# First attention of a fused transformer kernel: value products of four heads issued together in four 32-column groups

## The chip, the cores and the metric

The kernel runs on one core of one Trainium2 chip as one launch. The metric is the device time of that launch in microseconds (us), as a median of runs; lower is better.

## The reference, cut to what matters

The program is a four-layer model over 8 sequences (batches) of T = 333 tokens and width 256. An image tokeniser makes the first 256 tokens, 77 text tokens are appended, and four attention-like and four feed-forward-like layers follow. The change touches only the first attention, 16 heads of width 16, dense softmax, no mask:

```python
h = jnp.concatenate([h, txt], axis=1)
h = h + _L0_attn_ref(_layernorm(h, axis=-1), L0_attn_ln_g, L0_attn_ln_b, L0_attn_Wq, L0_attn_bq, ...)
# per batch and head:  softmax(q k^T / sqrt(16)) v      (q, k, v: 333 x 16)
```

## The kernel before, in words

Every engine runs its own instruction list, and the lists wait for one another through counted semaphores (`wait_ge`, `then_inc`). The first attention is the function `attention16`. The 333 tokens are three tiles of 111 (`NT = 3`), the 16 heads are 8 pairs (`NPAIR`), so a batch has `NS = 24` steps. In a step `s`, TensorE (PE), VectorE (DVE) and ScalarE (ACT) work on one pair and one tile each:

- `scores`, L719: PE writes query-by-key scores of a pair to one of two `psS` buffers, `AHEAD = 9` steps before they are needed.
- `largest`, L554: DVE reduces them to the row maximum into `mx`. After six steps a `most` piece turns the maxima on PE (L702) and DVE makes `mT` out of them (`mhigh` L580, `mT` L582).
- `scores_less_most`, L731 and L734: PE computes the turned scores (keys by queries) and adds minus the maximum, into the single buffer `psT`. When `s % 6 == 0` it first waits for the `most` piece of its four heads. It always waits for the `exp` of the step before.
- `exp`, L653: ACT reads `psT` and writes probabilities to `PT`.
- `values`, L745: PE multiplies the probabilities with `vS` and accumulates in `psO`, 32 output columns to a head. One float32 product is two MATMUL records in the trace, so a step's two heads are four. `out` (L657, ACT) copies `psO` after four heads.

Between these, PE works off *pieces* that all share the one buffer `psM`: `x` (L687, turned input of the next batch), `qk` (L691, projections), `v` (L697), `most` (L702), `ot` (L706, turned output). A piece on PE waits until its predecessor was read out of `psM` (`piece_out`). ACT reads out `x` and `qk`; DVE reads out `v` (L575), `most` (L580, L582) and `ot` (L586, L589). Their places among the steps are a list written out by hand:

```python
AT = [(1, "x", 0), (2, "x", 1), (3, "qk", 0), (4, "qk", 1), (5, "most", 1), (6, "ot", 3), (7, "qk", 2),
      (8, "qk", 3), (9, "ot", 0), (11, "most", 2), (12, "v", 0), (13, "v", 1), (15, "ot", 1), (17, "most", 3),
      (21, "ot", 2), (23, "most", 0)]
```

The first batch has no `("ot", 3)`; the last has only `most` 1 to 3 and `ot`. Batches 1 to 6 run in a hardware loop of three rounds with two batches each. DVE's list for a step is unchanged by the diff and reads:

```python
if s + AHEAD < NS or not last:
    largest(*of(b, p, s + AHEAD)[::2])
for args in pieces(b, p, s, first, last):
    piece(*args)
```

Of the kernel before, what the change touches and what calls it, by code (L numbers as in the profile page):

```python
# [21 lines left out]
ACT = mybir.ActivationFunctionType  # L22
# [3 lines left out]
T = 333  # L26
TT = 111
NT = 3
# [337 lines left out]
def attention16(nc, sh):  # L366
# [5 lines left out]
    H, DH = 16, 16  # L372
    NPAIR = 8
    NS = NPAIR * NT
    TE = T + 1
    HIGH = -4096
    AHEAD = 9
    with ExitStack() as ctx:
        sb = lambda name, shape, dt=F32: ctx.enter_context(nc.sbuf_tensor(name, shape, dt))
# [15 lines left out]
        spread = sb("spread", [128, 2, TT], F32R)  # L395
        sign = sb("sign", [128, 2])
        less = sb("less", [128, 1])
        PT = [sb(f"PT{i}", [TT, 2, NT, T]) for i in range(2)]
        oS = sb("oS", [128, T])
        rec = sb("rec", [TT, NT, 4])  # L400
        tmp = sb("tmp", [TT, NT, 4, DH])
# [54 lines left out]
        def some(n):  # L456

            return not isinstance(n, int) or n > 0

        def of(b, p, s):  # L460

            return (b, p, s) if s < NS else (b + 1, 1 - p, s - NS)

# [167 lines left out]
        @block.scalar  # L631
        def _(act):
            s_ = nc.scalar

            def piece(kind, j, b, p, n):
                if kind == "x":
                    act.wait_ge(piece_done, n + 1)
                    s_.activation(xT[:, j, :], psM[:, 0:T], ACT.Identity, bias=sh.col("a_b", j),
                                  scale=sh.col("a_g", j)).then_inc(piece_out, 1)
                if kind == "qk":  # L640
                    act.wait_ge(piece_done, n + 1)
                    if some(4 * b + j - 1):
                        act.wait_ge(low_ready, 4 * b + j - 1)
                    bias, scale = (bq4[:, j // 2:j // 2 + 1], DH ** -0.5) if j % 2 == 0 else (sh.col("a_bk", j // 2), 1.0)
                    s_.activation(raw[j % 2][:, :], psM[:, 0:T], ACT.Identity, bias=bias,
                                  scale=scale).then_inc(piece_out, 1)

            def exp(b, s):
                jp, a = s // NT, s % NT
                act.wait_ge(st_done, NS * b + s + 1)  # L650
                if a == 0 and some(NPAIR * b + jp - 1):
                    act.wait_ge(pv_done, NPAIR * b + jp - 1)
                s_.activation(PT[jp % 2][:, :, a, :], psT[0:TT, :, 0:T], ACT.Exp).then_inc(exp_done, 1)  # L653

            def out(b, g):
                act.wait_ge(pv_done, NPAIR * b + 2 * g + 2)
                s_.activation(oS[:, :], psO[:, 0:T], ACT.Copy).then_inc(o_out, 1)  # L657

            act.wait_ge(consts, 3)
            for n, (kind, j) in enumerate(START):  # L660
                piece(kind, j, 0, 0, n)

            def body(b, p, first, last):
                for s in range(NS):
                    if s == 1 and not first:
                        out(b - 1, 3)
                    if s % 6 == 1 and s > 1:
                        out(b, s // 6 - 1)
                    for args in pieces(b, p, s, first, last):
                        piece(*args)  # L670
                    exp(b, s)
                if last:
                    out(b, 3)
            batches(act, body)

        @block.tensor
        def _(pe):
            mm = nc.tensor.matmul

            def piece(kind, j, b, p, n):  # L680
                if some(n):
                    pe.wait_ge(piece_out, n)
                if kind == "x":
                    if j == 0:
                        pe.wait_ge(xn_ready, b + 1)
                    for t in range(NT):
                        r = nc.tensor.transpose(psM[:, qt(t)], xn[:, t, 128 * j:128 * j + 128], sh.ident[0:TT, 0:TT])  # L687
                if kind == "qk":
                    at = 128 * (j // 2)
                    for c in range(KT):  # L690
                        r = mm(psM[:, 0:T], sh.wt("a_q" if j % 2 == 0 else "a_k", c, at, at + 128), xT[:, c, :],  # L691
                               start=c == 0, stop=c == KT - 1)
                if kind == "v":
                    for t in range(2 * j, min(2 * j + 2, NT)):
                        at = D * (t % 2)
                        for c in range(KT):
                            r = mm(psM[0:TT, at:at + D], xT[:, c, qt(t)], sh.wt("a_v", c, 0, D),  # L697
                                   start=c == 0, stop=c == KT - 1, skip_group_check=True)
                if kind == "most":
                    pe.wait_ge(mx_ready, 4 * b + j + 1)  # L700
                    for t in range(NT):
                        r = nc.tensor.transpose(psM[:, qt(t)], mx[j % 2][:, t, :], sh.ident[0:TT, 0:TT])  # L702
                if kind == "ot":
                    pe.wait_ge(o_out, 4 * b + j + 1)
                    for t in range(NT):
                        r = nc.tensor.transpose(psM[0:TT, 128 * t:128 * t + 128], oS[:, qt(t)], sh.ident[:, :])  # L706
                r.then_inc(piece_done, 1)

            def scores(b, p, s):

                jp, t = s // NT, s % NT
                if t == 0 and jp % 4 == 0:
                    for n in (jp // 2, jp // 2 + 1):
                        pe.wait_ge(stack_in[n], 128 * (b + 1))
                if some(NS * b + s - 1):
                    pe.wait_ge(max_done, NS * b + s - 1)
                for half in range(2):
                    ph = slice(64 * half, 64 * half + 64)
                    r = mm(psS[s % 2][0:TT, half, 0:TE], qs[p][ph, jp, qt(t)], ks[p][ph, jp, :], start=True, stop=True)  # L719
                r.then_inc(s_done, 1)  # L720

            def scores_less_most(b, p, s, first, last):

                jp, a = s // NT, s % NT
                if s % 6 == 0:
                    pe.wait_ge(piece_out, most_place(b, jp // 2, first, last) + 1)
                if some(NS * b + s):
                    pe.wait_ge(exp_done, NS * b + s)
                for half in range(2):
                    ph = slice(64 * half, 64 * half + 64)  # L730
                    mm(psT[0:TT, half, 0:TE], ks[p][ph, jp, qt(a)], qs[p][ph, jp, :], start=True, stop=False)  # L731
                for half in range(2):
                    ph = slice(64 * half, 64 * half + 64)
                    r = mm(psT[0:TT, half, 0:TE], spread[ph, jp % 2, :], mT[jp // 2 % 2][ph, :], start=False, stop=True)  # L734
                r.then_inc(st_done, 1)

            def values(b, p, s):
                jp, a = s // NT, s % NT
                pe.wait_ge(exp_done, NS * b + s + 1)
                if s % 6 == 0 and some(4 * b + jp // 2):  # L740
                    pe.wait_ge(o_out, 4 * b + jp // 2)
                for half in range(2):
                    h = 2 * jp + half
                    at = 32 * (h % 4)
                    r = mm(psO[at:at + 32, 0:T], vS[p][:, a, h, :], PT[jp % 2][:, half, a, :], start=a == 0,  # L745
                           stop=a == NT - 1)
                if a == NT - 1:
                    r.then_inc(pv_done, 1)

            for n, (kind, j) in enumerate(START[:-1]):  # L750
                if n == 0:
                    pe.wait_ge(consts, 3)
                piece(kind, j, 0, 0, n)
            for s in range(AHEAD):
                scores(0, 0, s)
            piece("most", 0, 0, 0, N0 - 1)

            def body(b, p, first, last):
                for s in range(NS):
                    if s + AHEAD < NS or not last:  # L760
                        scores(*of(b, p, s + AHEAD))
                    if s >= 2:
                        values(b, p, s - 2)
                    elif not first:
                        values(b - 1, 1 - p, NS + s - 2)
                    for args in pieces(b, p, s, first, last):
                        piece(*args)
                    scores_less_most(b, p, s, first, last)
                if last:
                    values(b, p, NS - 2)  # L770
                    values(b, p, NS - 1)
                    piece(*tail())
            batches(pe, body)


# [2268 lines left out]
```

## Time and profile before

| | us |
|---|---|
| median of three runs | 2289.98 (2289.2 to 2295.62) |
| the profiled execution, its own time | 2287.08 |
| its span in the trace | 2285.3 |
| PE busy (matmul) | 1807.9, 79% of the span |
| DVE busy | 1140.6, 50% |
| ACT busy | 759.1, 33% |

PE is TensorE's matmul stream and PEld its weight loads. A row of the timeline has the start in us from the start of the span, the duration in us, engine, source line, operation, output<-inputs with shapes, and how many instructions were merged into it; in brackets stands how long the engine was idle before and what released it. Matmul ends are modelled, so the start of the next instruction is the better measure of when PE was free. PEclk is the granted TensorE clock as a share of 2.4 GHz. The first attention's steps run from about 167 us to 540 us.

### The profile page before, as it was taken

How to read it: one execution, taken by the hardware profiler on the slowest of the kernel's cores; microseconds unless marked ns; L12 is line 12 of the kernel's file. 1: busy time of each engine (PE TensorE's matmuls, PEld its weight loads, DVE VectorE, ACT ScalarE, POOL GpSimd, SP SyncE). 2: the span in 40 equal slices, each digit the busy share in tenths (PEclk: the TensorE clock that was granted, in tenths of full speed). 3: DMA queues.
4: the chain of work that ended last, by engine and by line, in shares of the span. 5: the costliest groups of instructions: out<-in, count | busy, mean ns of one | idle time of the engine just before them, and what ended most of it. 6: DMA issues, size and time to landing. Idle time of an engine off the chain costs nothing. (4 is left out here: it accounts for less than half of the span.)

```text
span 2285.3 us, 32329 instructions
## 1 busy us (share of the span) xinstructions
PE 1807.9 (79%) x9490; PEld 1178.8 (52%) x9490; DVE 1140.6 (50%) x3699; ACT 759.1 (33%) x1873; POOL 502.2 (22%) x728
## 2 busy tenths in 40 slices
PE   0049999998897989777763999768888888882998
PEld 0024444444665667554541677535666555661676
DVE  5346767673326766744552222156665666641111
ACT  0004444453231245221210221137555566630211
POOL 0130100001101122301111111114434444531122
PEclk9999999998997999899885999859998999995999
DMA  8444544444200000160000101030000010002332
GB/s 179 133 79 89 106 81 87 72 72 121 84 18 0 1 1 1 39 257 12 12 13 24 33 30 33 26 106 9 16 17 19 24 25 19 19 19 59 129 135 70
DMA packets 72299, 129.65 MB, mean 57 GB/s; under 512 B 23030, under 2 KB 59573, under 8 KB 67442
## 3 DMA queue, kind: packets, MB, share of 16 engines
q1 hardware_dynamic: 52636, 107.80, 18.1%
q0 software_dynamic: 17632, 14.26, 2.5%
q10 hardware_dynamic: 1893, 5.99, 0.8%
q8 instruction: 56, 0.92, 0.2%
q14 instruction: 82, 0.67, 0.1%
HBM read 89.79 MB, written 39.52 MB: 57 GB/s over the span
## 5 line engine op out<-in xcount | busy, mean ns | idle before, releaser
L2304 POOL TENSOR_SCALAR l_P<-l_P,l_ri 111x111 f32<-111x111 f32 (+1 forms) x256 | 178.3, 714 | 159.3 <-DVE l_ri L2492 158.4
L653 ACT ACTIVATE PT<-psT 111x666 f32<-111x666 f32 x192 | 139.4, 726 | 156.4 <-PE psT L734 156.0
L2586 ACT ACTIVATE l_P<-l_S,l_nm 111x111 f32<-111x111 f32 (+2 forms) x384 | 179.3, 471 | 32.7 <-DVE l_nm L2485 32.5
L554 DVE TENSOR_REDUCE mx<-psS 111x2 f32<-111x666 f32 x192 | 159.6, 847 | 25.7 <-PE psS L719 25.7
L745 PE MATMUL psO<-PT,vS 111*32 111x333 f32 x768 | 147.0, 461 | 0.1
L2706 PE MATMUL l_psP<-ident,l_P 111*111 111x111 f32 x768 | 108.8, 281 | 32.2 <-DVE l_PT L2501 27.6
L2706 PEld LDWEIGHTS l_psP<-ident,l_P 111*111 111x111 f32 x768 | 95.4, 189 | 62.9 <-issue 33.1
L2042 DVE COPY t_hT<-t_psG 128x512 f32<-128x512 f32 x56 | 36.1, 686 | 175.0 <-PE t_psG L2085 175.0
L2485 DVE CUSTOM_DVE_ANT_0 l_S<-l_psA,l_am 111x111 f32<-111x111 f32 (+1 forms) x256 | 79.0, 331 | 76.9 <-PE l_psA L2692 70.1
L2074 PE MATMUL t_psH<-expert_w,t_xT 128*128 x224 | 103.4, 606 | 1.5 <-DVE t_xT L2035 1.2
L2097 PE MATMUL t_psY<-expert_w,t_hT 128*128 x448 | 101.4, 379 | 0.6 <-ACT t_yb L2007 0.6
L2595 ACT ACTIVATE l_P<-l_P,l_ri 111x333 f32<-111x333 f32 x128 | 66.2, 565 | 90.5 <-DVE l_ri L2492 90.4
L2718 PE MATMUL l_psO<-l_PT,l_vS 111*64 111x333 f32 (+2 forms) x768 | 95.8, 388 | 0.6 <-ACT l_oT L2600 0.6
L521 POOL TENSOR_TENSOR low<-raw,high 128x333 f32<-128x333 f32 x32 | 28.6, 895 | 307.6 <-DVE high L566 307.6
L2677 PE MATMUL l_psM<-l_wo,l_oT 128*111 128x256 f32 x384 | 87.7, 381 | 8.5 <-ACT l_oT L2600 7.5
L106 DVE BATCH_NORM_STATS2 moments<-h 111x6 f32<-111x256 f32 (+1 forms) x192 | 69.1, 416 | 42.0 <-DMA h<-h_scratch 36.5
L2097 PEld LDWEIGHTS t_psY<-expert_w,t_hT 128*128 128x128 f32 x448 | 82.9, 190 | 11.1 <-issue 1.0
L2928 PE MATMUL c_psY<-c_w,c_hT 128*111 128x256 f32 x384 | 84.2, 379 | 0.6 <-DVE c_yb L2875 0.6
L687 PE MATMUL psM<-ident,xn 111*128 111x111 f32 x48 | 10.6, 343 | 92.7 <-DVE spread L611 82.5
L2911 PE MATMUL c_psH<-c_xT,c_w 128*128 128x333 f32 x256 | 76.8, 459 | 8.6 <-DVE c_xT L2861 6.5
L731 PE MATMUL psT<-qs,ks 64*111 64x334 f32 x384 | 79.4, 409 | 3.2 <-DVE mT L582 0.7
L2718 PEld LDWEIGHTS l_psO<-l_PT,l_vS 111*64 111x64 f32 x768 | 53.6, 148 | 52.0 <-issue 19.2
(401 smaller groups left out, 3744.4 us busy)
## 6 DMA issues: line engine op xcount, KB each, us to landing
expert_w<-in_moe_dram SPq DMA_DIRECT2D x8, 2048.0 KB, 24.6
c_w<-in_moe_dram SPq DMA_DIRECT2D x16, 1024.0 KB, 7.2
qs<-halves_scratch SPq DMA_DIRECT2D x128, 83.5 KB, 3.2
ks<-halves_scratch SPq DMA_DIRECT2D x128, 83.5 KB, 4.1
halves_scratch<-high SPq DMA_DIRECT2D x32, 167.0 KB, 3.0
halves_scratch<-low SPq DMA_DIRECT2D x32, 167.0 KB, 3.6
c_xb<-xs_scratch SPq DMA_DIRECT2D x8, 667.3 KB
xs_scratch<-zeros SPq DMA_DIRECT2D x6, 777.0 KB
```

The lines of the kernel that those rows point to most:

```text
L554: v.tensor_reduce(mx[J % 2][:, t, c:c + 65:64], psS[s % 2][0:TT, :, 0:T], AX.X, ALU.max, negate=True).then_inc(max_done, 1)
L653: s_.activation(PT[jp % 2][:, :, a, :], psT[0:TT, :, 0:T], ACT.Exp).then_inc(exp_done, 1)
L731: mm(psT[0:TT, half, 0:TE], ks[p][ph, jp, qt(a)], qs[p][ph, jp, :], start=True, stop=False)
L745: r = mm(psO[at:at + 32, 0:T], vS[p][:, a, h, :], PT[jp % 2][:, half, a, :], start=a == 0, stop=a == NT - 1)
L2074: r = mm(psH[s % 2][q][:, :], xT[s % 2][:, k, :], experts.w[:, e, 1024 * k + 512 * q:1024 * k + 512 * q + 512], start=k == 0, stop=k == KT ...
L2097: r = mm(psY[:, 0:D], hT[s % 2][:, c, :], experts.w[:, e, at:at + D], start=c == 0, stop=c == 7)
L2304: r = g.tensor_scalar(Pt, Pt, ri[:, c % 2, 2 * t + half:2 * t + half + 1], None, ALU.mult)
L2586: s_.activation(P[c % 4][:, half, at(t):at(t + 1)], Sm[:, half, at(t):at(t + 1)], ACT.Exp, bias=nm[:, c % 2, i:i + 1], scale=-1.0, accum_o ...
L2677: r = mm(psM[0:TT, 0:D], oT[p][:, c, qt(j)], wo[:, c, :], start=c == 0, stop=c == NC - 1)
L2706: r = nc.tensor.transpose(psP[0:TT, half, qt(i)], P[c % 4][:, half, at(t) + TT * a:at(t) + TT * a + TT], sh.ident[0:TT, 0:TT])
L2718: r = mm(psO[64 * half:64 * half + 64, TT * a:T], vS[p][:, a, DH3 * kv:DH3 * kv + DH3], PT[c % 2][:, half, a, TT * a:T], start=a == 0, sto ...
L2928: r = mm(psY[t % 2][0:TT, 0:D], hT[p][:, f, qt(t)], stream.w[p][:, at:at + D], start=f == 0, stop=f == NF - 1)
```

## The change

`values` no longer runs once in a step for two heads and one key tile, but once in two steps for four heads and one key tile: eight MATMUL records into the four 32-column groups of `psO`. For that, a batch's steps are renumbered on the exp side: `parts(s)` makes even and odd steps the first and second pair of the same four heads on the same key tile, where before the three tiles of one pair followed each other. `PT` becomes three buffers (one to a tile) of two pairs each. Semaphore counts follow. PE's order in a step changes too: before it was scores, values, pieces, scores less most; now it is pieces, scores less most, scores, and values in even steps. ACT's and DVE's orders stay.

```diff
+    NQ = NS // 2
-        PT = [sb(f"PT{i}", [TT, 2, NT, T]) for i in range(2)]
+        PT = [sb(f"PT{i}", [TT, 2, 2, T]) for i in range(NT)]
+        def parts(s):
+            return 2 * (s // 6) + s % 2, s % 6 // 2
...
             def exp(b, s):
-                jp, a = s // NT, s % NT
+                jp, a = parts(s)
                 act.wait_ge(st_done, NS * b + s + 1)
-                if a == 0 and some(NPAIR * b + jp - 1):
-                    act.wait_ge(pv_done, NPAIR * b + jp - 1)
-                s_.activation(PT[jp % 2][:, :, a, :], psT[0:TT, :, 0:T], ACT.Exp).then_inc(exp_done, 1)
+                if some(NQ * b + s // 2 - 2):
+                    act.wait_ge(pv_done, NQ * b + s // 2 - 2)
+                s_.activation(PT[a][:, jp % 2, :, :], psT[0:TT, :, 0:T], ACT.Exp).then_inc(exp_done, 1)
             def out(b, g):
-                act.wait_ge(pv_done, NPAIR * b + 2 * g + 2)
+                act.wait_ge(pv_done, NQ * b + NT * g + NT)
...
-            def values(b, p, s):
-                jp, a = s // NT, s % NT
-                pe.wait_ge(exp_done, NS * b + s + 1)
-                if s % 6 == 0 and some(4 * b + jp // 2):
-                    pe.wait_ge(o_out, 4 * b + jp // 2)
-                for half in range(2):
-                    h = 2 * jp + half
-                    at = 32 * (h % 4)
-                    r = mm(psO[at:at + 32, 0:T], vS[p][:, a, h, :], PT[jp % 2][:, half, a, :], start=a == 0,
-                           stop=a == NT - 1)
-                if a == NT - 1:
-                    r.then_inc(pv_done, 1)
+            def values(b, p, u):
+                J, a = u // NT, u % NT
+                pe.wait_ge(exp_done, NS * b + 2 * u + 2)
+                if a == 0 and some(4 * b + J):
+                    pe.wait_ge(o_out, 4 * b + J)
+                for c in range(2):
+                    for half in range(2):
+                        n = 2 * c + half
+                        r = mm(psO[32 * n:32 * n + 32, 0:T], vS[p][:, a, 4 * J + n, :], PT[a][:, c, half, :],
+                               start=a == 0, stop=a == NT - 1)
+                r.then_inc(pv_done, 1)
...
                 for s in range(NS):
-                    if s + AHEAD < NS or not last:
-                        scores(*of(b, p, s + AHEAD))
-                    if s >= 2:
-                        values(b, p, s - 2)
-                    elif not first:
-                        values(b - 1, 1 - p, NS + s - 2)
                     for args in pieces(b, p, s, first, last):
                         piece(*args)
                     scores_less_most(b, p, s, first, last)
+                    if s + AHEAD < NS or not last:
+                        scores(*of(b, p, s + AHEAD))
+                    if s % 2 == 0:
+                        if s >= 2:
+                            values(b, p, s // 2 - 1)
+                        elif not first:
+                            values(b - 1, 1 - p, NQ - 1)
```

## Rows read from the trace of the kernel before

**Rows 1.** Windows view, first attention: us, busy per engine (instructions), PEclk, DMA share, GB/s.
```profile
170.00:538.00 368.00, 355.40 (x2305) 167.33 (x2301) 253.75 (x607) 171.97 (x262) 32.13 (x42) 0.98 0.43 79
```

**Rows 2.** Timeline of a step without a piece, then the next one's start.
```profile
504.87 0.41 PE L731 MATMUL psT<-qs,ks 64*111 64x334 f32 x2
...
505.11 0.32 PE L734 MATMUL psT<-mT,spread 64*111 64x334 f32 x2
...
505.26 0.32 PE L719 MATMUL psS<-ks,qs 64*111 64x334 f32 x2
505.47 0.73 ACT L653 ACTIVATE PT<-psT 111x666 f32<-111x666 f32 x1 [0.66 <-PE psT L734]
...
505.51 0.75 PE L745 MATMUL psO<-PT,vS 111*32 111x333 f32 x4
505.62 0.85 DVE L554 TENSOR_REDUCE mx<-psS 111x2 f32<-111x666 f32 x1 [0.26 <-PE psS L719]
...
506.25 0.41 PE L731 MATMUL psT<-qs,ks 64*111 64x334 f32 x2
```

**Rows 3.** Timeline of the last batch's end, where no scores are left.
```profile
536.15 0.40 PE L731 MATMUL psT<-qs,ks 64*111 64x334 f32 x2
...
536.63 0.75 PE L745 MATMUL psO<-PT,vS 111*32 111x333 f32 x4
...
537.52 0.17 PEld L731 LDWEIGHTS psT<-qs,ks 64*111 64x111 f32 x2 [0.75 <-ACT PT L653]
```

**Rows 4.** PE's timeline over batch 6: each kind of piece, and a batch's period.
```profile
450.90 0.75 PE L745 MATMUL psO<-PT,vS 111*32 111x333 f32 x4
451.59 0.58 PE L706 MATMUL psM<-ident,oS 128*111 128x128 f32 x3
452.10 0.41 PE L731 MATMUL psT<-qs,ks 64*111 64x334 f32 x2
...
454.80 0.50 PE L702 MATMUL psM<-ident,mx 111*128 111x111 f32 x3
...
456.71 0.41 PE L731 MATMUL psT<-qs,ks 64*111 64x334 f32 x2
...
464.20 1.39 PE L691 MATMUL psM<-xT,w 128*128 128x333 f32 x4
...
480.69 1.98 PE L697 MATMUL psM<-w,xT 128*111 128x256 f32 x8
...
483.93 1.12 PE L697 MATMUL psM<-w,xT 128*111 128x256 f32 x4
...
502.11 0.40 PE L731 MATMUL psT<-qs,ks 64*111 64x334 f32 x2
```

**Rows 5.** Timeline of steps 5 and 6: a `most` piece, then an `ot` piece.
```profile
324.22 0.41 PE L731 MATMUL psT<-qs,ks 64*111 64x334 f32 x2
...
324.32 0.51 DVE L580 TENSOR_SCALAR mhigh<-psM 128x333 int32<-128x333 int32 x1
...
324.91 0.57 DVE L582 SCALAR_TENSOR_TENSOR mT<-psM,less,mhigh 128x333 fp32r<-128x333 f32 x1
...
325.60 0.57 PE L706 MATMUL psM<-ident,oS 128*111 128x128 f32 x3
...
326.22 0.23 DVE L586 RECIPROCAL rec<-psM 111x12 f32<-111x12 f32 x1
...
326.53 0.49 DVE L589 TENSOR_TENSOR tmp<-psM,rec 111x64 f32<-111x64 f32 x3
```

**Rows 6.** Timeline of step 12: DVE reads out the first `v` piece.
```profile
482.71 0.76 DVE L575 TENSOR_TENSOR vS<-psM,rows 111x256 f32<-111x256 f32 x2 [1.33 <-PE psM L697]
```

**Rows 7.** Timeline after the hardware loop's second round began, TensorE at its low clock.
```profile
312.96 1.32 PE L745 MATMUL psO<-PT,vS 111*32 111x333 f32 x4
```

**Rows 8.** Windows view, two stretches of later stages with PE partly idle.
```profile
580.00:590.00 10.00, 7.15 (x24) 5.17 (x25) 2.71 (x2) 3.70 (x8) 2.25 (x1) 0.83 0.19 78
...
670.00:680.00 10.00, 6.79 (x24) 4.31 (x24) 2.47 (x3) 3.03 (x6) 0.00 (x0) 1.00 0.00 0
```

More of the change, by code:

```diff
@@ L722, in scores_less_most @@
             def scores_less_most(b, p, s, first, last):
-                jp, a = s // NT, s % NT
+                jp, a = parts(s)
                 if s % 6 == 0:
@@ L735, in scores_less_most @@
                 r.then_inc(st_done, 1)
-            def values(b, p, s):
-                jp, a = s // NT, s % NT
-                pe.wait_ge(exp_done, NS * b + s + 1)
-                if s % 6 == 0 and some(4 * b + jp // 2):
-                    pe.wait_ge(o_out, 4 * b + jp // 2)
-                for half in range(2):
-                    h = 2 * jp + half
-                    at = 32 * (h % 4)
-                    r = mm(psO[at:at + 32, 0:T], vS[p][:, a, h, :], PT[jp % 2][:, half, a, :], start=a == 0,
-                           stop=a == NT - 1)
-                if a == NT - 1:
-                    r.then_inc(pv_done, 1)
+            def values(b, p, u):
[9 more added lines that the diff above has]
+                r.then_inc(pv_done, 1)
             for n, (kind, j) in enumerate(START[:-1]):
@@ L768, in body @@
                     scores_less_most(b, p, s, first, last)
+                    if s + AHEAD < NS or not last:
[5 more added lines that the diff above has]
+                            values(b - 1, 1 - p, NQ - 1)
                 if last:
-                    values(b, p, NS - 2)
-                    values(b, p, NS - 1)
+                    values(b, p, NQ - 1)
                     piece(*tail())
```

## The prediction

> **What bounds the kernel now.** I read the busy shares by window first: in the first attention PE is busy 355.4 of 368 us and DVE 253.8 [rows 1], at a granted clock of 0.98 [rows 1]. That looks like a plain PE bound, so I read the timeline step by step, because a step has two limits that happen to meet. I time a step from one L731 to the next.
>
> The first limit is PE's own work [rows 2]: L731 to L734 0.24 us, to the scores L719 0.15, to the values L745 0.25, together 0.65; then the values. In front of a piece the values hold PE for 0.69 us (450.90 to 451.59) [rows 4]. A piece is worth its listed duration less 0.07, as the next instruction starts that much before the modelled end (`ot` 0.58 listed, 0.51 to the next) [rows 4]: `x` and `most` 0.44 (both are three turns of 111 columns), `ot` 0.51, `qk` 1.32, `v0` 1.91, `v1` 1.05.
>
> The second limit is the turn between PE and ACT over the one buffer `psT` [rows 2]: L731 starts at 504.87, exp at 505.47 (0.60 later), runs 0.73, and the next L731 follows at 506.25, 0.05 after its end. That is 1.38 us, whatever else PE does. The end of the last batch shows it alone: no scores are left there, PE is done with the values at 536.63 + 0.69 = 537.32, and still the next L731 waits for ACT until 537.52, 1.37 us after the one before [rows 3]. So a step without a piece is bound by exp's turn, with PE's 0.65 + 0.69 = 1.34 just underneath; a step with a piece is bound by PE. A middle batch takes 502.11 - 456.71 = 45.4 us [rows 4]. Eight steps of 1.38 and sixteen of 1.34 plus their piece (2 `x`, 4 `qk`, 4 `most`, 4 `ot`, 2 `v` = 12.9) give 45.4, so the two limits explain the batch.
>
> **The change part by part (times are for a middle batch).**
>
> *Values in four groups.* Two heads take 0.75 us for four records with a mean near 0.46, so two groups do run side by side, in two passes of about 0.28. Four groups are not in the trace. Lower bound 0.69 (all hidden), upper bound 0.69 + 2 x 0.28 = 1.25 (two and two). I take 0.75, near the lower, since the second group adds no pass of its own: the added 0.06 is for four more starts.
> The Trainium skill's "TensorE: Matmul & The Clock Gate" (section Measured speedup vs the span model) gives about 4 ns to a further tile of a packed group; by that the block would be 0.70, and the sum below 4 us lower (an estimate).
>
> *What the saved blocks are worth.* In an odd step no values stand on PE any more. It needs 0.40 + about 0.26 plus the next piece. But exp's 1.38 stays, so a step without a piece gains nothing: the twelve saved blocks are mostly turned into PE idle time. It pays only where a piece that is done before an even step is PE-bound now: s = 1 (`x1`) 1.78 to 1.38, s = 3 and 7 (`qk`) 2.66 to 1.98. Gain 0.40 + 2 x 0.68 = 1.8. Eleven of sixteen pieces stand in front of odd steps, right behind the values of an even one, and gain nothing; nine of these pay the 0.06 of the larger block (s = 0, 2, 4, 8, 10, 14, 16, 20, 22), and s = 18 0.03: cost 0.6.
> A rule that speaks against the change stands in "TensorEngine Tiling (Array Packing)" of the Trainium skill (PSUM Bottleneck): tiling makes TensorE faster but not the reading out of PSUM. The trace agrees, with 1.38 us for exp's turn.
>
> *PE's new order against DVE's old one.* This is the term that decides. DVE's list of a step is largest(s+9), then piece(s). Before, PE issued scores(s+9) ahead of piece(s), so that reduction was done or running when the piece came. Now scores(s+9) comes after the piece and after L731/L734. DVE, in order, can't read out piece(s) until those scores are there and reduced. From L731 of step s: scores start at 0.40, the reduction 0.36 after that (505.26 to 505.62) and takes 0.85 [rows 2]: 1.61 us. Only then comes the piece's read-out, which before began 0.1 us after L731 (324.22 to 324.32) [rows 5]. Where something on PE waits for that read-out soon, PE stalls:
>
> - `most`: `mhigh` to the end of `mT` is 1.16 us (324.32 to 325.48) [rows 5]. Ready at 1.61 + 1.16 = 2.77. A next `psM` piece starts 0.12 later (325.60), at 2.89. An L731 that waits for `mT` starts 0.21 after it: at s = 23 the step takes 1.47 now (454.80 + 0.44 to 456.71) [rows 4], of which 0.10 and 1.16 are before the end of `mT`. So 2.98.
> - s = 17 and 23: the next L731 has s % 6 = 0 and waits for `mT`. 1.47 to 2.98, +1.51 each.
> - s = 5: `ot3` waits for `psM`, 2.89 + 0.51 = 3.40, before 1.34 + 0.51 = 1.85: +1.55.
> - s = 11: `v0` waits, 2.89 + 1.91 = 4.80, before 1.34 + 1.91 = 3.25: +1.55.
> - s = 6: `qk2` waits for `ot3`'s read-out, 0.80 us (326.22 to 327.02) [rows 5]: 1.61 + 0.80 + 0.12 + 1.32 = 3.85, before 2.66: +1.19.
> - s = 12: `v1` waits for `vS`, 0.76 [rows 6]: 1.61 + 0.76 + 0.12 + 1.05 = 3.54, before 2.39: +1.15. Its larger values block is covered here, as in s = 6.
>
> Together 8.5. The other `ot` pieces have two or more steps before the next piece: covered. `x` and `qk` are read out by ACT, whose order against PE stays.
>
> *Buffers and waits.* exp waits for values two groups back, out waits for the last block of its four heads, which ends some 1.4 us into an even step, and its 0.45 us are over by 1.9, before the odd step's exp can start at 1.98. Nothing. If that cover went, 0.4 us four times a batch. The `scores` keep 8 steps of lead; their reduction waits for no one else.
>
> Sum for a middle batch: 8.5 + 0.6 - 1.8 = +7.3, six times: 43.8. The first batch has no `ot3`: s = 5 still waits for `mT` (+1.51), s = 6 doesn't stall: 3 x 1.51 + 1.55 + 1.15 + 0.6 - 1.8 = +6.0. The last has no `x`, `qk`, `v`, and from s = 15 no reduction ahead of the piece: s = 5 (+1.5), s = 11 (+1.5), and 0.1: +3.1. Where TensorE is at its low level (1.2 GHz) behind a loop boundary and at the start, a values block costs 1.25 instead of 0.69 [rows 7]; one of the two blocks goes in three such places, and the piece steps gain some 1 us each: -3. Total 43.8 + 6.0 + 3.1 - 3 = +49.9.
>
> The profiled execution is 2287.1, so 2337.0; the median of the runs is 2.9 above it: about **2340 us**, 2.2% slower.
>
> **The rivals.**
>
> *PE's busy time is what counts (faster).* If exp's turn were shorter than 1.38 when PE is idle, and DVE's late read-outs found slack, each batch would lose twelve blocks of 0.69 less twelve times 0.06: 7.6 us, 60 us in all: 2230. For it: PE's 97% share [rows 1]. Against it: the 1.37 with PE idle [rows 3]. It needs both to hold; it decides once the stalls are under what the lighter PE saves.
> By the skill's "TensorE: Matmul & The Clock Gate" (the small-M row of its table) column groups give 2.38 times for three tiles; that speedup is of PE alone.
>
> *No change.* DVE's late read-out is hidden by something that I don't see, exp's turn stays: -1.8 + 0.6 a batch, about -10 at most: 2280 to 2290.
>
> *Four groups run two and two.* Ten even steps a batch pay 0.5 more: +5 a batch, 40 in all: 2381.
>
> *The clock.* After the change PE idles for some 2.2 us in s = 5, 11, 17 and 23, and in most odd steps 0.7. Elsewhere a window with 7.15 of 10 us busy was granted 0.83, one with 6.79 busy 1.00 [rows 8]. So dips can come or not. A dip of 3.4 us (0.83 over 10 us) makes about 1.5 us of loss, by 1.32 against 0.75 for the values [rows 7, 4]; two a batch 24 us: 2365.
>
> **How the numbers follow.** Chances: forecast 0.70, two and two 0.09, clock 0.11, no change 0.04, faster 0.06. About 0.3% (7 us) is what can be told from no change here. Slower by more: 0.90; within: 0.04; faster: 0.06. The range takes the forecast with each stall up to a third smaller (8.5 to 5.7, about 20 us: 2320) up to two-and-two with a few dips, 2388.
>
> **What would show it.** Right: a batch's period of L731 near 52.7 us; DVE's `mhigh` 1.6 us after L731 instead of 0.1; idle PE before L706, L697, L691 and L731 released by DVE `mT`, `tmp`, `vS`, about 50 us more than now; steps without a piece still 1.38; exp count and duration unchanged. Wrong: `mhigh` right behind its piece; no-piece steps below 1.38; L745's eight records spanning more than 1 us; PEclk well below 0.98 over the stage. The code's order on DVE is the thing I lean on most; the four-group block is the least known size.

## The result and the profile after

The changed kernel takes 2398.6 us (median of four, 2386.8 to 2405.1) against 2292.4: a ratio of 1.0457, 95% interval 1.041 to 1.0504. Slower, as forecast, but by 106 us and not by 50, and above the stated range (up to 2388). The profiled execution is 2401.9 us, span 2400.2.

The profile's page gives the granted clock in 40 slices of 60 us, in tenths. Slices 3 to 11 hold the first attention:

```profile
PEclk9988777878599899999886699977998999986999
```

The windows view from the first L736 (the L731 of before) of the first attention to the last; columns as in [rows 1]:

```profile
165.73:646.16 480.43, 374.18 (x2315) 191.83 (x2315) 256.94 (x612) 175.44 (x264) 32.11 (x42) 0.76 0.33 61
```

The same stretch of before, cut at the same two instructions, is 370.2 us. So nearly all of the difference (110 of 115 us of span) is in this stage. Its mean granted clock fell from 0.98 [rows 1] to 0.76, which is about half of the time at the low level of 1.2 GHz.

The timeline of two steps at the high level: first step 20 of the seventh batch, then its step 23, which ends with the wait of step 0 of the last batch. L724 are the scores, L750 the values, L711 an `ot` piece and L707 a `most` piece:

```profile
587.41 0.41 PE L736 MATMUL psT<-qs,ks 64*111 64x334 f32 x2 [0.67 <-ACT PT L658]
...
588.05 0.77 PE L750 MATMUL psO<-PT,vS 111*32 111x333 f32 x8
588.75 0.58 PE L711 MATMUL psM<-ident,oS 128*111 128x128 f32 x3
```
```profile
591.97 0.51 PE L707 MATMUL psM<-ident,mx 111*128 111x111 f32 x3
592.40 0.40 PE L736 MATMUL psT<-qs,ks 64*111 64x334 f32 x2
...
592.79 0.31 PE L724 MATMUL psS<-ks,qs 64*111 64x334 f32 x2
...
593.92 0.50 DVE L585 TENSOR_SCALAR mhigh<-psM 128x333 int32<-128x333 int32 x1
594.49 0.57 DVE L587 SCALAR_TENSOR_TENSOR mT<-psM,less,mhigh 128x333 fp32r<-128x333 f32 x1
...
595.11 0.40 PE L736 MATMUL psT<-qs,ks 64*111 64x334 f32 x2 [2.00 <-DVE mT L587]
```

Eight records in four column groups hold PE for 0.70 us (588.05 to 588.75), no longer than four did in two [rows 4]. And `mhigh` begins 1.52 us after L736, where it was 0.10 [rows 5]: PE is idle for 2.00 us until `mT` is there.

The same kind of steps at the low level, in the sixth batch (steps 22 and 23):

```profile
533.19 1.34 PE L750 MATMUL psO<-PT,vS 111*32 111x333 f32 x8
534.46 0.82 PE L707 MATMUL psM<-ident,mx 111*128 111x111 f32 x3
...
535.21 0.62 PE L736 MATMUL psT<-qs,ks 64*111 64x334 f32 x2
...
538.38 0.62 PE L736 MATMUL psT<-qs,ks 64*111 64x334 f32 x2 [2.00 <-DVE mT L587]
```

The same work takes PE 1.5 to 1.8 times as long as above: 0.62 for 0.41 (L736), 0.82 for 0.51 (L707), 1.34 for 0.77 (L750). The wait for `mT` is 2.00 us at either level. The waits from 160 to 650 us (waiting engine and line, what it waited for: us, times, longest):

```profile
DVE mx L559 <- PE psS L724: 184.4, 152, 4.0
...
PE psT L736 <- DVE mT L587: 33.6, 17, 2.1
...
PE psT L736 <- ACT PT L658: 28.4, 45, 0.9
...
PE psM L711 <- DVE mT L587: 14.3, 7, 2.1
PE psM L702 <- DVE mT L587: 14.0, 7, 2.0
```

DVE waits for the scores that now come late, and PE waits for DVE. In the stage of before, DVE waited for the scores for 24.7 us, PE waited for `mT` only once, for 0.7 us, and for ACT's exp once, for 0.2.

All of this is best read as step lengths, L736 to L736, steps 0 to 23 of the fifth batch, worked out from the timelines (the last row is e3, experiment 4 below; each length can be off by 0.01):

```
before  1.76 1.76 2.65 2.64 1.75 1.84 2.64 2.64 1.83 1.38 1.76 3.23 2.38 1.39 1.85 1.38 1.75 1.47 1.46 1.38 1.84 1.38 1.75 1.47 = 45.4
after   3.12 1.84 3.44 2.12 1.77 3.23 4.88 3.56 1.84 1.39 1.78 4.62 3.37 1.37 1.85 1.38 1.77 2.72 1.46 1.54 3.29 1.71 3.13 3.14 = 60.3
filled  1.78 1.40 2.67 2.11 1.78 3.22 3.67 2.10 1.84 1.38 1.78 4.62 3.36 1.38 1.85 1.38 1.77 2.72 1.45 1.38 1.85 1.37 1.77 (4.77, loop boundary)
```

The steps 5, 11, 12 and 17 are the forecast's waits. Steps 6 and 23 have such a wait too, but are longer than it makes them, and 19 to 22, 0 to 2 and 7 are long with no such wait at all: that is the clock.

### The profile page after: what moved, and what is told of

The parts are those of the page before. It is cut to its first block and busy times, and to the rows that moved or that the text cites. A ratio compares the mean times of both kernels' runs of the same rounds, so it can differ in the third digit from the quotient of the medians.

```text
span 2400.2 us, 32450 instructions
## 1 busy us (share of the span) xinstructions
PE 1828.2 (76%) x9490; PEld 1205.0 (50%) x9490; DVE 1141.8 (48%) x3699; ACT 760.3 (32%) x1873; POOL 500.8 (21%) x728
## 5 line engine op out<-in xcount | busy, mean ns | idle before, releaser
L736 PE MATMUL psT<-qs,ks 64*111 64x334 f32 x384 | 94.5, 488 | 62.1 <-DVE mT L587 33.6
L736 PEld LDWEIGHTS psT<-qs,ks 64*111 64x111 f32 x384 | 39.8, 204 | 132.4 <-ACT PT L658 55.5
L750 PE MATMUL psO<-PT,vS 111*32 111x333 f32 x768 | 95.3, 576 | 0.8 <-ACT PT L658 0.8
L106 DVE BATCH_NORM_STATS2 moments<-h 111x6 f32<-111x256 f32 (+1 forms) x192 | 69.1, 415 | 41.6 <-DMA h<-h_scratch 36.2
## 6 DMA issues: line engine op xcount, KB each, us to landing
expert_w<-in_moe_dram SPq DMA_DIRECT2D x8, 2048.0 KB, 24.7
```

The source lines that it names most:

```text
L750: r = mm(psO[32 * n:32 * n + 32, 0:T], vS[p][:, a, 4 * J + n, :], PT[a][:, c, half, :], start=a == 0, stop=a == NT - 1)
```

## The experiments

The theory after the result was this: DVE's late read-outs make the waits; the waits together with the lighter PE draw the clock down; and the clock costs more than the waits. The rival theory: the packing alone (PE idle in every odd step) draws the clock down, and the waits have nothing to do with it. Ratios are against the kernel before in the same job, with 95% intervals. The kernels are called e1 to e10, and the expectations count them so (the fifth kernel is e5). Granted clocks and step lengths are those of one profiled run of each.

**1. Scores ahead of the pieces again, four-head values kept (e1).**

```diff
                 for s in range(NS):
+                    if s + AHEAD < NS or not last:
+                        scores(*of(b, p, s + AHEAD))
+                    if s % 2 == 1:
+                        if s >= 3:
+                            values(b, p, (s - 3) // 2)
+                        elif not first:
+                            values(b - 1, 1 - p, NQ - 1)
                     for args in pieces(b, p, s, first, last):
                         piece(*args)
                     scores_less_most(b, p, s, first, last)
-                    if s + AHEAD < NS or not last:
-                        scores(*of(b, p, s + AHEAD))
-                    if s % 2 == 0:
...
```

Expected: 

> The changed kernel with PE's scores back in front of the pieces (four-head values kept). Order theory (DVE's read-outs came late because the scores came after the piece, and the waits that follow also drew TensorE's clock down): mhigh starts 0.1 us behind its piece again, no waits for mT, vS or tmp over 0.3 us, PEclk of the stage back to 0.95 or more, 2280 to 2292 us. Packing theory (PE's idle 0.7 us in odd steps lowers the clock by itself): the waits go, but PEclk stays near 0.75 in the stage and the time at 2320 to 2350.

2280.7 us, ratio 0.9928 (0.9903 to 0.9953): 0.7% below the kernel before, and at the lower end of what the order theory gave. The stage's windows view and a `most` piece of its timeline:

```profile
166.69:531.66 364.97, 302.65 (x2312) 159.98 (x2312) 256.06 (x612) 174.21 (x264) 32.15 (x42) 0.96 0.44 80
```
```profile
387.01 0.41 PE L736 MATMUL psT<-qs,ks 64*111 64x334 f32 x2
...
387.12 0.51 DVE L585 TENSOR_SCALAR mhigh<-psM 128x333 int32<-128x333 int32 x1 [0.15 <-PE psM L707]
...
388.48 0.41 PE L736 MATMUL psT<-qs,ks 64*111 64x334 f32 x2 [0.76 <-ACT PT L658]
```

`mhigh` is back at 0.11 us behind L736, the step at 1.47, the clock at 0.96, with PE busy 303 of 365 us only. So the packing doesn't draw the clock down in the middle batches. One of them takes 44.1 us against 45.4. The profiled stage is 5 us shorter than before, while the medians differ by 15. The profiled run (2288.2) was slower than its median, and outside the stage it is 6 us longer than the profile of before, so it can't show where the rest of the 15 lies.

**2. DVE's read-outs ahead of its reduction, PE as changed (e4).**

```diff
+                    for args in pieces(b, p, s, first, last):
+                        piece(*args)
                     if s + AHEAD < NS or not last:
                         largest(*of(b, p, s + AHEAD)[::2])
-                    for args in pieces(b, p, s, first, last):
-                        piece(*args)
```

Expected: 

> The changed kernel with DVE's read-out of a piece put ahead of its reduction of the same step; PE untouched. If the order on DVE is the cause: no waits over 0.3 us for mT, vS or tmp, and 2280 to 2295 us, the same as with the scores first. If the lateness comes from elsewhere: within 15 us of the changed kernel's 2398.

2286.4 us, 0.9973 (0.994 to 1.0006), no different from before. Two swapped lines on an engine whose list the change didn't touch take away 112 us. Step 17 of the fifth batch in PE's timeline:

```profile
388.59 0.40 PE L736 MATMUL psT<-qs,ks 64*111 64x334 f32 x2
...
390.07 0.41 PE L736 MATMUL psT<-qs,ks 64*111 64x334 f32 x2 [0.77 <-ACT PT L658]
```

`mhigh` starts 0.11 us behind the first of them, and the second waits for exp and no longer for `mT`. The cause of the waits is the order of the two lists against each other, on whichever side it is mended. A middle batch is 44.2. The last is 46.7 against 38.0 of e1 in the profiled runs, much of it at the low clock (experiments 8 and 9).

**3. The new order alone, with two heads a step (e2).**

```diff
                 for s in range(NS):
-                    if s + AHEAD < NS or not last:
-                        scores(*of(b, p, s + AHEAD))
-                    if s >= 2:
-                        values(b, p, s - 2)
-                    elif not first:
-                        values(b - 1, 1 - p, NS + s - 2)
                     for args in pieces(b, p, s, first, last):
                         piece(*args)
                     scores_less_most(b, p, s, first, last)
+                    if s + AHEAD < NS or not last:
+                        scores(*of(b, p, s + AHEAD))
+                    if s >= 1:
+                        values(b, p, s - 1)
+                    elif not first:
+                        values(b - 1, 1 - p, NS - 1)
...
```

Expected: 

> The kernel before with the new order on PE alone (pieces, scores less most, scores, values of the step before; still two heads a step). Order theory: the waits behind DVE's late read-outs are there in full, about 8 us a batch, 55 to 65 us in all at full clock; with the clock falling behind them as in the changed kernel, 2360 to 2400. Packing theory: the waits without a fall of the clock (PE has its values in every step), 2345 to 2355, PEclk of the stage 0.95 or more.

2358.3 us, 1.0294 (1.0252 to 1.0336).

```profile
170.24:603.71 433.47, 371.24 (x2316) 173.50 (x2316) 256.29 (x612) 174.04 (x264) 32.18 (x42) 0.94 0.36 68
```

The long steps are there with the same lengths (steps 5, 6, 11, 12, 17: 3.23, 3.68, 4.62, 3.37, 2.72 in the fifth batch), but the clock holds at 0.94. The time lies between what the two theories gave for it: the late read-outs cost 63 us, and the clock does not fall far. But PE's own idle time in these steps isn't the same. PE has two heads' values in each of them, and they fill 0.7 us of the wait. At the end of the same step 17:

```profile
439.21 0.41 PE L731 MATMUL psT<-qs,ks 64*111 64x334 f32 x2 [1.32 <-DVE mT L582]
```

So e2 has neither the waits of 2.00 us nor the idle odd steps of the changed kernel, and it can't tell which of the two the low clock needs.

**4. The changed kernel with PE kept busy in the waits (e3).** 12 pairs of matmuls of no use go into the free `psS` buffer in steps 5, 11, 17 and 23, except in the last batch.

```diff
+            def fill(b, p, s):
+                pe.wait_ge(max_done, NS * b + s + AHEAD)
+                for i in range(12):
+                    for half in range(2):
+                        ph = slice(64 * half, 64 * half + 64)
+                        mm(psS[(s + AHEAD + 1) % 2][0:TT, half, 0:TE], spread[ph, 0, :], ks[p][ph, NPAIR - 1, :],
+                           start=True, stop=True)
...
+                    if s in (5, 11, 17, 23) and not last:
+                        fill(b, p, s)
```

Expected: 

> The changed kernel with 12 pairs of matmuls of no use (fp32r, into the free psS buffer) behind the scores in steps 5, 11, 17 and 23, about 1.8 us at full clock, inside PE's waits of 2 us. If PE's idleness in those waits is what draws the clock down: PEclk of the stage back above 0.9, 2335 to 2360 us though PE has more to do. If the fall has another cause: PEclk as in the changed kernel (0.75 in the stage), time 2395 or more, as the filler itself takes twice as long at the low clock.

2339.6 us, 1.02 (1.0153 to 1.0247): 59 us less than the changed kernel, by adding work, and inside the first range of the expectation. The first fence is step 17 of the seventh batch in PE's timeline, with the filler as L747, the second the stage:

```profile
528.78 0.40 PE L736 MATMUL psT<-qs,ks 64*111 64x334 f32 x2
...
529.43 2.08 PE L747 MATMUL psS<-ks,spread 64*111 64x334 f32 x24
531.50 0.41 PE L736 MATMUL psT<-qs,ks 64*111 64x334 f32 x2
```
```profile
167.15:588.62 421.47, 362.97 (x2986) 211.29 (x2986) 256.37 (x612) 173.96 (x264) 32.26 (x42) 0.94 0.37 71
```

The step is as long as without the filler (2.72), and the clock is 0.94. What the filler gave back is the clock, not the wait. The last batch, which has no filler, still falls: 46.6 us.

**5 to 7. Which waits draw it down, and how little filler does.** As in 4, with the filler only in steps 17 and 23 (e6), only in steps 5 and 11 (e7), and in all four with 4 pairs for 12 (e10).

Expected of e6: 

> The changed kernel with the filler of no use only in steps 17 and 23, whose waits have a sparse stretch of PE between them. If these two draw the clock down: steps 18 to 24 and 0 to 3 back at full clock, 2345 to 2370. If the pair of waits in steps 5 and 6 does it: 2385 or more.

Expected of e7: 

> The changed kernel with the filler only in steps 5 and 11. If the waits of steps 17 and 23 draw the clock down: 2375 to 2395, with steps 18 to 24 still long. If step 5 does it: 2345 to 2360.

Expected of e10: 

> The changed kernel with 4 instead of 12 pairs of no use in steps 5, 11, 17 and 23 (0.6 us of waits of some 1.3 to 2 us). If any shortening of the idle time brings the clock back: 2335 to 2350, as with 12 pairs. If what counts is how much of the stretch PE is busy: between the changed kernel and the one with 12 pairs, 2355 to 2385, with steps 18 to 24 low in some batches.

| filler | median us | ratio (interval) | stage's clock |
|---|---|---|---|
| none (changed kernel) | 2398.6 | 1.0457 (1.041 to 1.0504) | 0.76 |
| steps 5, 11 | 2381.6 | 1.038 (1.034 to 1.042) | 0.82 |
| steps 17, 23 | 2361.6 | 1.0292 (1.0264 to 1.032) | 0.91 |
| all four | 2339.6 | 1.02 (1.0153 to 1.0247) | 0.94 |
| all four, 4 pairs | 2339.2 | 1.0179 (1.015 to 1.0208) | 0.89 |

The late pair accounts for 37 us, the early one for 17, and 54 is near the 59 of both. e6 and e7 came out as their first answers said. With 17 and 23 filled, steps 18 to 23 are back (1.45, 1.38, 1.85, 1.38, 1.78, 2.71), and 0 to 3 with them, while 6 and 7 stay long (4.88, 3.62); with 5 and 11 filled it is mostly the other way round. It isn't strict: in e6 the clock also falls at step 11 in three batches (5.54 for 4.62 in two of them), and one batch of e7 keeps it through steps 18 to 23 without filler there.

A third of the filler (e10) does as much by the medians, the first answer of its expectation. Its profile was taken in its slowest run (2358.3, in the range of the second answer), so its clock isn't that of the median. This profile shows something more. The filler takes 0.7 us of each wait, and the waits that are left are 1.2 to 1.4 us, as in e2; the odd steps still have their 0.67 us of idle time. Step 17 of the third batch ends so:

```profile
322.85 0.41 PE L736 MATMUL psT<-qs,ks 64*111 64x334 f32 x2 [1.21 <-DVE mT L587]
```

The second and third batch of this run (230.56 to 333.47 us) have a granted clock of 1.00 throughout. So idle odd steps together with waits of 1.2 to 1.4 us need not bring it down, and the length of the waits seems to matter too; other batches of the same run do fall, so it is not settled.

**8. Pieces moved to even steps, on top of e1 (e5).**

```diff
-        AT = [(1, "x", 0), (2, "x", 1), (3, "qk", 0), (4, "qk", 1), (5, "most", 1), (6, "ot", 3), (7, "qk", 2),
-              (8, "qk", 3), (9, "ot", 0), (11, "most", 2), (12, "v", 0), (13, "v", 1), (15, "ot", 1), (17, "most", 3),
-              (21, "ot", 2), (23, "most", 0)]
+        AT = [(1, "x", 0), (2, "x", 1), (3, "ot", 3), (4, "qk", 0), (5, "most", 1), (6, "qk", 1), (8, "qk", 2),
+              (9, "ot", 0), (10, "qk", 3), (11, "most", 2), (12, "v", 0), (14, "v", 1), (15, "ot", 1),
+              (16, "most", 3), (20, "ot", 2), (22, "most", 0)]
```

Expected: 

> Scores first and four-head values as in the first run, with the pieces' list changed so that as many as can be stand in even steps, in front of which PE has no values. By the two limits of a step (PE's own sum, exp's turn of 1.38) a middle batch takes 41.7 us against 44.4 there: about 19 us less, 2258 to 2268. If the saved blocks are worth nothing because exp's turn hides PE in every step, or if the clock falls with the idleness, 2275 to 2290.

2277.1 us, 0.9926 (0.9899 to 0.9952): not separable from e1, and in the second range of the expectation. A middle batch takes 43.1 us at best, not 41.7. Its steps 13 to 23 are at 1.37 to 1.87 as worked out, but step 5 is 3.6 to 5.0 in all middle batches but one (2.6), as DVE has `ot` 3 with its statistics just before. And the last batch takes 45 us, against 35.4 before, mostly at the low clock. PE's timeline there, where it has no projections (scores go on until step 14); the first row is the end of step 5, the others are steps 9 and 10:

```profile
492.72 0.41 PE L736 MATMUL psT<-qs,ks 64*111 64x334 f32 x2 [1.40 <-DVE mT L587]
...
499.30 0.62 PE L736 MATMUL psT<-qs,ks 64*111 64x334 f32 x2
...
501.01 0.62 PE L736 MATMUL psT<-qs,ks 64*111 64x334 f32 x2 [0.54 <-ACT PT L658]
...
502.12 1.34 PE L750 MATMUL psO<-PT,vS 111*32 111x333 f32 x8
```

The fall comes right behind a wait of 1.40 us for `mT` (the values at 493.37 already take 1.00 us), so e5 doesn't show what the packing does alone. The last batch of e1 shows more of it:

```profile
505.50 0.40 PE L736 MATMUL psT<-qs,ks 64*111 64x334 f32 x2 [0.67 <-ACT PT L658]
...
506.82 0.41 PE L724 MATMUL psS<-ks,qs 64*111 64x334 f32 x2 [0.77 <-DVE mx L559]
507.16 0.95 PE L750 MATMUL psO<-PT,vS 111*32 111x333 f32 x8
```

L750 is the first long record; in the 13 us before it no wait of PE was longer than 0.77 us. The kernel before has a wait of 0.74 us at the same place and keeps the clock at 1.00 through its last batch. So the rival theory has its part: where PE has no projections left, the packing lets the clock fall with short waits only.

**9. The same with 4 pairs of filler in even steps of the last batch (e8), and 10. `ot` 3 back in step 6, `qk` 0 and 1 in 3 and 4 (e9).** e8 is e5 with this filler. In e9 the list is `(3, "qk", 0), (4, "qk", 1), (5, "most", 1), (6, "ot", 3), (8, "qk", 2)`, the rest as in e8, its filler included.

Expected of e8: 

> The fifth kernel with 4 pairs of matmuls of no use in each even step of the last batch, where PE has neither scores nor projections. If PE's idleness alone draws the clock down there: the last batch at full clock, 5 to 15 us less than the fifth where that one's last batch fell to the low clock, 2250 to 2262. If the fall has another cause: no difference, or some us more.

Expected of e9: 

> The eighth kernel (pieces in even steps, filler in the last batch) with ot 3 back in step 6 and qk 0 and 1 back in steps 3 and 4. There DVE has ot 3 with its statistics at step 3 and is late for the most piece of step 5, which makes step 5 3.65 us; by the step lengths seen so far a middle batch goes from 43.1 to 41.8, 2260 to 2268 us. If the statistics are late for something else as well in step 6: no change, 2270 to 2278.

e8: 2274.5 us, 0.9915 (0.9888 to 0.9942). In its profile the last batch is 35.7 us at a clock of 1.00:

```profile
485.00:518.00 33.00, 30.76 (x305) 18.50 (x301) 20.84 (x58) 17.07 (x25) 1.04 (x2) 1.00 0.01 1
```

The profiled stages differ by 8 us as expected, but the medians by 2.7 with overlapping runs, and 2274.5 is far from the 2250 to 2262 that was expected: the effect is shown in the profile, not in the times. The filler also covers the wait in step 5, so e8 doesn't part that wait from the packing. e9: 2273.1 us, 0.9895 (0.9874 to 0.9917). Step 5 is back at 1.82 to 1.90, but steps 8 and 9 grew to 2.43 to 2.62 and 2.59. In the timeline DVE's statistics push its reductions back, for which the scores of step 8 wait 0.34 us, and then the read-out of `ot` 0, for which `qk` 3 waits 0.56. A middle batch is 42.8, not 41.8, and the time lies in the second range of its expectation.

e1, e5, e8 and e9 are 0.7 to 1.1% below the kernel before, and are hardly told apart.

## Why the prediction was right in its direction and wrong in its size

*Two limits of a step, exp's turn of 1.38: right.* Steps without a piece are 1.37 to 1.39 after, PE idle for 0.67 in the odd ones. With the order mended, the packing is worth 1.3 us a batch (e1), forecast 1.8 - 0.6 = 1.2. Both terms were too large and make up for one another: steps 1, 3 and 7 gained 0.35, 0.53 and 0.54, not 0.40, 0.68 and 0.68, and the larger blocks cost 0.1 in all, not 0.6. The rival that counted PE's busy time (2230) is excluded: in e1 PE was busy for 303 us of the stage against 358 before, and the stage was 5 us shorter.
The Trainium skill's "TensorEngine Tiling (Array Packing)" (PSUM Bottleneck) says that tiling doesn't speed up reading out PSUM; the trace agrees, with exp's turn at 1.38 us still.

*Values in four groups: right at the lower bound.* 0.70, taken as 0.75. The two-and-two rival is excluded.
By the Trainium skill's "TensorE: Matmul & The Clock Gate" (Measured speedup vs the span model), about 4 ns for each further tile, the block was to be 0.70 (an estimate); the trace agrees.

*DVE's late read-outs: right in place and mechanism, somewhat too large.* Steps 5, 6, 11, 12 and 17 are 3.22, 3.67, 4.62, 3.37 and 2.72 at the high clock; forecast were 3.40, 3.85, 4.80, 3.54 and 2.98. `mhigh` starts at 1.52, not 1.61, as a next DVE instruction starts before the reduction's listed end, and the read-out's end reaches a waiting L736 in 0.05, not 0.21. A middle batch at the high clock is 51.3 us (each step at its full-clock length in the changed kernel and the filled ones) against 52.7 forecast: +5.9, not +7.3. e1 and e4 show the cause from both sides, e2 shows that the order alone suffices.

*The clock: the step that failed.* The sum held nothing for what the new idle time does to the clock; it was a rival with a chance of 0.11 and a price of 24 us. Of the stage's +110 us, the lengths at the high clock give about 44 (six middle batches of 5.9, 5.2 for the first, some 3 for the last). The other 66 (an estimate from these lengths) are the low clock, and the filler of e3 gave back 59. A middle batch has 5 to 11 us of it (60.3 against 51.3 in the fifth), in steps 19 to 23, 0 to 2, 6 and 7, which take 3.29 for 1.85 (step 20), 3.13 for 1.77 (22), 4.88 for 3.67 (6). The rival's mechanism was the right one, and a clock well below 0.98 stood among the forecast's signs of being wrong. The rival's price was made from dips of 3.4 us as one later stage showed [rows 8]; here a fall that sets in behind step 17 lasts some eight steps, through the next wait in step 23. That the recurring waits keep it down fits e6 and e7, where filling one pair of them mostly frees its own stretch and not the other's. The forecast's rival already listed the idle times (2.2 us in four steps, 0.7 in most odd ones; measured 2.00 and 0.67), but the sum took them as free.

That the filled kernel (e3) lands on the forecast's 2340 is partly chance: waits too large by some 9 us stand against a low clock in its last batch (46.6 us against 35.4 before).

*Interaction.* The parts do not add. Order alone (e2): +63 us. Packing alone, in the old order (e1): -15. Both: +106. The 58 that are too many go with the clock, which held with the late read-outs alone (0.94) and with the lighter PE alone (0.96), and not with both (0.76). Both together do two things: PE's waits grow from 1.3 to 2.0 us, as no values stand in them, and the steps between have idle time. e10 speaks for the length of the waits, e1's last batch for the idle time between; no run here parts the two.

Open are which of the two brings the clock down, and where e1's gain stands beyond the 5 us that its profile shows.

## What to carry to other kernels

When a producer's order is changed, lay every consumer's list beside it: an in-order engine that has A before B makes B late by the whole of A as soon as A's input comes after B's. Price a saved block by the step's other limit first; here the saved PE time became idle time. A change that leaves TensorE waiting in several places needs a clock term in its sum, not a rival beside it; a few matmuls of no use in the waits (59 us back in e3) tell how much of a loss is clock.

## What the hardware showed that was not expected

The clock fell though no wait of PE was longer than 2.00 us. PE's timeline of the changed kernel in the third batch: the wait of step 11, then the L736 of steps 16, 18 and 19. Between them lie waits of 0.91 us (step 12) and 0.67 (step 14). The L736 of step 19 is the first long one:

```profile
318.24 1.98 PE L702 MATMUL psM<-w,xT 128*111 128x256 f32 x8 [2.00 <-DVE mT L587]
...
328.13 0.41 PE L736 MATMUL psT<-qs,ks 64*111 64x334 f32 x2 [0.67 <-ACT PT L658]
...
332.61 0.41 PE L736 MATMUL psT<-qs,ks 64*111 64x334 f32 x2 [2.00 <-DVE mT L587]
...
333.25 0.77 PE L750 MATMUL psO<-PT,vS 111*32 111x333 f32 x8
334.07 0.62 PE L736 MATMUL psT<-qs,ks 64*111 64x334 f32 x2
```
```profile
319.00:338.00 19.00, 14.15 (x110) 7.22 (x108) 10.90 (x23) 7.43 (x11) 0.00 (x0) 0.89 0.31 44
338.00:346.00 8.00, 6.54 (x36) 3.50 (x32) 3.73 (x12) 2.18 (x3) 0.00 (x0) 0.50 0.01 2
```

The fall lies inside the first of these two windows, at 334.07: cut there, the view gives a clock of 1.00 from 319 us on, with PE busy for 10.76 of 15.07 us, and 0.50 up to 346, with PE busy for 9.93 of 11.93. PE's busy share is the higher one at the low level, as the same work then fills more of the time.

One wait of 2 us need not do it. In the last batch of e9, where the other even steps have filler, PE waits 1.99 us in step 7, and the granted clock is 1.00 over the whole batch (36.2 us):

```profile
496.88 0.86 PE L747 MATMUL psS<-ks,spread 64*111 64x334 f32 x8 [1.99 <-DVE mx L559]
```

And 0.7 us of filler in each of four waits a batch was worth 59 us (e10).
